# Expert feed-forward on sorted blocks instead of on all experts, in a one-core decoder layer

## The reference

```python
scores = (einsum('btd,ed->bte', x, router_w) + router_b) / max(temperature, 0.1)
gates  = sinkhorn(scores)      # 3 times: subtract logsumexp over experts (-1), then over tokens (-2);
                               # then exp, and divide by the row sum
topk_vals, topk_idx = top_k(gates, 2)
topk_gates = topk_vals / (sum(topk_vals) + 1e-8)
g = relu(einsum('btd,edf->btef', x, wg));  p = einsum('btd,edf->btef', x, wp)
all_out = einsum('btef,efd->bted', g * p, wo)
expert_out = sum(take(all_out, topk_idx) * topk_gates)
x = layernorm(x + (x + expert_out))
```

## Time and profile before

| | |
|---|---|
| median of the runs | 1088.37 us |
| span of the profiled execution | 1083.9 us |
| PE busy | 1014.5 us (94%), 7692 matmuls |
| DVE busy | 775.1 us (72%) |
| ACT busy | 701.3 us (65%) |
| POOL busy | 514.4 us (47%) |
| DMA moved | 14.46 MB, mean 13 GB/s |

### The profile page before, as it was taken

The page is one execution under the profiler, slowest core; times in us unless marked ns, Lnnn a source line. Parts: engine busy times, 40 slices in busy tenths (PEclk is TensorE's granted clock), DMA queues, the critical chain, the costliest instruction groups (busy, mean ns, idle before and its releaser), DMA issues. The chain is left out here.

```text
span 1083.9 us, 24953 instructions
## 1 busy us (share of the span) xinstructions
PE 1014.5 (94%) x7692; PEld 821.1 (76%) x7692; DVE 775.1 (72%) x2061; ACT 701.3 (65%) x2313; POOL 514.4 (47%) x777
## 2 busy tenths in 40 slices
PE   5999999999999999999999999995399999999996
PEld 3677777777778777777777777773288888888886
DVE  3688888888888888888888888885386445544554
ACT  4787888878888788888888888872832222222221
POOL 4744565455654556545665456630323233323333
PEclk9999999999999999999999999996599999999999
DMA  4000000000000000000000000000300000000000
GB/s 116 9 8 11 8 12 7 7 10 7 12 7 7 10 10 10 7 7 10 11 9 7 7 10 10 5 2 0 117 1 10 1 10 10 10 0 10 10 10 10
DMA packets 22520, 14.46 MB, mean 13 GB/s; under 512 B 3296, under 2 KB 21472, under 8 KB 22240
## 3 DMA queue, kind: packets, MB, share of 16 engines
q1 hardware_dynamic: 22496, 14.15, 4.4%
HBM read 12.05 MB, written 2.10 MB: 13 GB/s over the span
## 5 line engine op out<-in xcount | busy, mean ns | idle before, releaser
L1063 ACT ACTIVATE gs<-ps 128x512 f32<-128x512 f32 x128 | 76.4, 599 | 208.7 <-PE ps L1259 208.7
L409 ACT ACTIVATE prob<-ps,negmax 128x128 f32<-128x128 f32 x512 | 182.1, 420 | 1.2 <-DVE negmax L515 1.2
L417 ACT ACTIVATE xprob<-ps,xmax 128x128 f32<-128x128 f32 x512 | 145.5, 428 | 18.5 <-DVE xmax L515 18.5
L336 POOL TENSOR_TENSOR prob<-prob,recip 128x512 f32<-128x512 f32 x128 | 137.2, 1081 | 35.7 <-DVE recip L520 35.7
L1029 POOL TENSOR_TENSOR acc<-acc,part 128x512 f32<-128x512 f32 x64 | 82.6, 1290 | 143.0 <-DVE part L1192 141.2
L345 POOL TENSOR_TENSOR qk_sin<-qk,sin_sb 128x128 f32<-128x128 f32 x256 | 114.3, 466 | 70.9 <-ACT qk L397 70.5
L409 ACT ACTIVATION_READ_ACCUMULATOR prob<-ps,negmax 128x1 f32 x512 | 133.3, 260 | 0.0
L1267 PEld LDWEIGHTS ps<-fwo_sb,h 128*128 128x128 f32 x1024 | 124.0, 192 | 5.6
L1146 DVE TENSOR_TENSOR h<-ps,gs 128x512 f32<-128x512 f32 x128 | 87.6, 689 | 54.9 <-PE ps L1259 53.8
L1267 PE MATMUL ps<-fwo_sb,h 128*128 128x128 f32 x1024 | 124.4, 275 | 0.0
L360 POOL TENSOR_TENSOR ve<-mv,eps 128x1 f32<-128x1 f32 x64 | 12.1, 189 | 208.3 <-DVE mv L538 208.3
(11 more groups left out here) (163 smaller groups left out, 2396.1 us busy)
## 6 DMA issues: line engine op xcount, KB each, us to landing
xf<-in_x SPq DMA_DIRECT2D x32, 64.0 KB, 1.8
xres<-in_x SPq DMA_DIRECT2D x32, 64.0 KB, 1.7
cx<-in_ctx SPq DMA_DIRECT2D x32, 64.0 KB, 1.8
out_y<-yo SPq DMA_DIRECT2D x8, 256.0 KB, 2.3
fstage<-in_fwg SPq DMA_DIRECT2D x1, 1024.0 KB, 5.2
fstage<-in_fwp SPq DMA_DIRECT2D x1, 1024.0 KB, 7.4
qk<-in_wqkv SPq DMA_DIRECT2D x1, 768.0 KB, 4.6
prob<-in_wqkv SPq DMA_DIRECT2D x1, 768.0 KB, 5.8
```

The costliest lines, as they stand in the source:

```text
L336: nc.gpsimd.tensor_tensor(prob[:, n], prob[:, n], recip[:, n, :, None].broadcast_to([128, 4, S]), ALU.mult).then_inc(normed, 1)
L409: last = nc.scalar.activation(prob[:, n, j, :], bank(name)[:, j * S:(j + 1) * S], ACT.Exp, bias=negmax[:, n, j:j + 1], accum_out=sums[:, n ...
L417: last = nc.scalar.activation(xprob[:, n, g, :], bank(name)[:, g * S:(g + 1) * S], ACT.Exp, bias=xmax[:, n, g:g + 1])
```

## The change

The feed-forward is computed only for the two experts of each token. The 32 batches form three groups of 8, 12 and 12. For each group the router runs by itself (64 or 96 columns, one transpose each way). From the chosen experts it counts: a product with a triangular matrix gives each token's rank within its batch for its expert, one with ones the counts, scans give where each expert's rows begin, rounded up to 128. Each token's row of x2 is scattered twice into a DRAM buffer `placed`, to the rows of its two experts, by an indirect transfer of POOL for each batch and choice. A group of n batches has 2n + 7 blocks of 128 rows, whatever the counts: 23 + 31 + 31 = 85. A block is loaded by SP, transposed by PE, split into high and low parts (ACT, DVE), multiplied with both up weights of its expert (512 columns at once, addressed by a register that PE loads from the table `owner`), relu, product, transposed back, multiplied with wo, and stored to DRAM `answered`. POOL gathers the two answers of each token by indirect transfers; DVE multiplies and adds them, and normalises as before. All of it is written out as straight code, no loop. The routing of groups 1 and 2 is dealt out two stages at a time between the blocks (`ROUTED`), the joining of four batches at fixed blocks (`JOINED`, `FINISHED`).

In the attention phase the split of x2 goes, the weight loads and the clearing of `placed` stand in SP's turn 3, and ACT loads one table set that holds exp and ln before all else. The diff, cut to its core:

```diff
+        plan = Sparse([8, 12, 12])
@@ attention_phase, SP, turn 3
+                if isinstance(s, int) and s == 3:
+                    pair = fw_lo[:].bitcast(F32).rearrange("p (e a f) -> p e a f", e=E, a=2)
+                    for a_, src in enumerate((fwg, fwp)):
+                        sp.dma_start(pair[:, :, a_, :], src.rearrange("p (e f) -> p e f", e=E)).then_inc(f_loaded, 16)
+                    sp.dma_start(fwo_sb[:].rearrange("p (n d) -> p n d", d=D), fwo.rearrange("(n p) d -> p n d", p=128))\
+                        .then_inc(fo_loaded, 16)
+                    sp.wait_ge(const_ready, 5)
+                    for rows in placed:
+                        n = rows.shape[0] // 128
+                        sp.dma_start(rows.rearrange("(n p) d -> p n d", p=128), zeros[:, None, :].broadcast_to([128, n, D]))\
+                            .then_inc(cleared, 16)
@@ ACT
+            nc.scalar.preload_act_table_set("natural_log_exp_and_others")
@@ DVE
-                    split_x2(s, c)
                     add_bias(s, c)
@@ ffn_phase
+        ROUTED = {}
+        for k in range(20, STAGES):
+            ROUTED.setdefault((k - 20) // 2, []).append((1, k))
+        for k in range(STAGES):
+            ROUTED.setdefault(11 + k // 2, []).append((2, k))
+        JOINED = {0: 33, 1: 40, 2: 64, 3: 71, 4: 78}
+        FINISHED = {0: 37, 1: 44, 2: 68, 3: 75, 4: 82}
@@ SP
+            def load(i):
+                g, p = plan.group_of[i], i % NX
+                if i == plan.block0[g]:
+                    sp.wait_ge(scattered[g], 16 * 2 * plan.size[g])
+                wait(sp, xt_filled, i - NX + 1)
+                sp.dma_start(xg[p][:], placed[g][at_row:at_row + 128, :]).then_inc(xg_loaded[p], 16)
+            def store(i):
+                sp.wait_ge(y_done, i + 1)
+                sp.dma_start(answered[g][at_row:at_row + 128, :], ysb[i % NY][:]).then_inc(y_stored[i % NY], 16)
+            for i in range(3):
+                load(i)
+            for i in range(NB):
+                if i >= 2:
+                    store(i - 2)
+                if i + 3 < NB:
+                    load(i + 3)
+                ...
@@ POOL
+            def dispatch(g):
+                pool.wait_ge(cleared, 16 * G)
+                pool.wait_ge(rt_dve, dve_after(g, SLOT))
+                for b in range(plan.size[g]):
+                    for k in range(2):
+                        nc.gpsimd.indirect_dma_start(
+                            placed[g], bass.IndirectOffsetOnAxis(place[g][:, k, b:b + 1], 0), x2_all[:, plan.first[g] + b, :], None,
+                            bounds_check=plan.blocks[g] * 128 - 1, oob_is_err=False).then_inc(scattered[g], 16)
+            def gather(q):
+                g, b = plan.quads[q]
+                if b == plan.first[g]:
+                    for p in range(NY):
+                        pool.wait_ge(y_stored[p], 16 * stores_before(p, plan.block0[g] + plan.blocks[g]))
+                wait(pool, acc_step, 3 * (q - 1))
+                for j in range(FB):
+                    for k in range(2):
+                        nc.gpsimd.indirect_dma_start(yg[q % 2][:, k, j, :], None, answered[g], ...)
+            dispatch(0)
+            dispatch(1)
+            gather(0)
+            gather(1)
+            rstd(0)
+            rstd(1)
+            dispatch(2)
+            for q in range(2, len(plan.quads)):
+                ...
@@ ACT
+            split_x(0)
+            for i in range(NB + 1):
+                if i + 1 < NB:
+                    split_x(i + 1)
+                if i < NB:
+                    relu(i)
+                if i >= 1:
+                    hidden_back(i - 1)
+                for g, k in ROUTED.get(i, ()):
+                    route(g, k)
@@ DVE
+            for k in range(STAGES):
+                route(0, k)
+            for k in range(20):
+                route(1, k)
+            split_x(0)
+            for i in range(NB + 2):
+                if i + 1 < NB:
+                    split_x(i + 1)
+                if i < NB:
+                    hidden(i)
+                if i >= 2:
+                    answer(i - 2)
+                for g, k in ROUTED.get(i, ()):
+                    route(g, k)
+                ...
+            for q in range(len(JOINED), len(plan.quads)):
+                join(q)
+                if q > len(JOINED):
+                    normalise(q - 1)
+            normalise(len(plan.quads) - 1)
@@ PE
+            def x_transpose(i):
+                p = i % NX
+                pe.wait_ge(xg_loaded[p], 16 * (i // NX + 1))
+                wait(pe, lo_done, i)
+                nc.tensor.transpose(ps[:, XT, 0:128], xg[p][:], ident[:]).then_inc(xt_filled, 1)
+            def expert_up(i, at_col):
+                pe.wait_ge(lo_done, i + 1)
+                wait(pe, h_done, i - 1)
+                dst, p = ps[:, UP[i % 2], :], i % 2
+                hi, lo = fw_hi[:, bass.ds(at_col * 2, 2 * FF)], fw_lo[:, bass.ds(at_col * 2, 2 * FF)]
+                nc.tensor.matmul(dst, x_lo[p][:], hi, start=True, stop=False)
+                nc.tensor.matmul(dst, x_hi[p][:], hi, start=False, stop=False)
+                nc.tensor.matmul(dst, x_hi[p][:], lo, start=False, stop=True).then_inc(up_filled, 1)
+            x_transpose(0)
+            for i in range(NB + 2):
+                if i < NB:
+                    ...
+                    owners[i] = pe.value_load(owner[g][0:1, j:j + 1], min_val=0, max_val=(E - 1) * FF)
+                    if i + 1 < NB:
+                        x_transpose(i + 1)
+                    expert_up(i, owners[i])
+                if 1 <= i <= NB:
+                    hidden_back(i - 1)
+                if i >= 2:
+                    expert_down(i - 2, owners.pop(i - 2))
+                for g, k in ROUTED.get(i, ()):
+                    route(g, k)
```

699 lines of the change are left out of this document (407 added, 292 removed).

## The result

The changed kernel takes 1186.55 us (median of 4 runs, 1182.43 to 1191.15) against 1088.86 for the kernel before: a ratio of 1.091, 95% interval [1.088, 1.094]. The profiled execution has a span of 1180.6 us. One later run of the kernel before took 1441.17 us at a mean granted clock of 0.65; it is left out of every ratio here. The forecast was 1079, range 1030 to 1160: it named the wrong side, and the time lies outside the range.

What follows compares the result with a forecast made beforehand. PE was taken to bound attention and dense feed-forward. After the logits, 44.2 + 232.5 + 41.1 = 317.8 us against 325.5 before, less 2 of attention: span 1074.2, plus 4.5 outside it, forecast 1079 us, range 1030 to 1160.

Steps and rivals of the forecast that it cites:

- Attention: Attention stretch: DVE loses the copy and subtraction splitting x2 per batch, 2 us less; queued loads and clears cost 0.
- Head: From last logits to first block: routing chain 22.8 us, 16 scatters 17.6, landing 2.0, first load 1.8; 44.2 us.
- Splitting the weights: Head: splitting on ACT, four times about 1 us, with POOL subtractions of 2.3 us each, fits into the chain's waits.
- A block: One block of 128 rows: a chain over five queues, 2.3 us taken, against 1.48 us of PE array time.
- second path: Block, through PE's queue: issuing about 1.2 us, then the expert's register load at 1.1; 2.3 us.
- Loop: All 85 blocks: 195.5 us, drain turns 3, joins 15, routing 12, late scatters 7; 232.5 us.
- Tail: After the blocks: store landing, 24 gathers at 26.4 us, a wait of 1.2, landing, join, normalising, store; 41.1 us.
- POOL rival: Head, tail and blocks: indirect transfer costs above 1.1 us, 88 us for each us; at 1.7, 1132 us; chance 0.25.
- clock rival: Blocks: PE's clock stays at the low level after the head, 1149 us; chance 0.21.
- fast rival: Blocks and transfers: register load and transfers answer sooner, 1.95 us a block, transfers at 1.0; 1048 us; chance 0.09.
- memory path: Block: from x's arrival through answer store to the load queued behind it, 4.4 us shared by two blocks; 2.2 us.

Runs made afterwards that it cites:

- e_lead: Changed kernel with loads up to six blocks ahead instead of three and seven row buffers instead of four, transfers unpaced: 1091.73 us (one run).
- plain-transfer kernel: Changed kernel with every indirect transfer replaced by a plain GpSimd one of 64 KB, fixed rows, so no placing by expert: 1076.97 us (one run).
- b_table: Kernel before with only the combined exp and ln activation table, loaded once at the start: 1082.4 us, ratio 0.996.
- m3: Test kernel without the layer: m1's buffers kept in place, stages varying source, target, operands, semaphores and spacing of transfers: 457.4 us.
- m3b: m3 unchanged, a second time, on m1's first chip: 567.1 us against 457.4.
- e_warm: e_paced with two extra matmuls of 512 columns per block into an unread bank: 1128.66 us against 1130.62 (one run).
- m1: Test kernel without the layer: ten stages of 44 matmul products, each beside one other activity such as scatters, gathers or plain transfers: span 470.1 us.
- m1c: m1 unchanged, a third time, on m1's first chip: 473.9 us.
- m1b: m1 unchanged, once more, on a fourth chip: span 472.0 us against 470.1.
- a3: Changed kernel unchanged, a third time, on a fifth chip: 1183.74 us.
- m2: Test kernel without the layer: ten stages as in m1 but longer, on another chip: no stage held up, no total time given.
- e_paced: Changed kernel with indirect transfers of groups 1 and 2 and first five gathers let go in pairs by finished blocks: 1130.62 us, ratio 1.040.
- e_final: e_lead with indirect transfers beside blocks four at a time, group 2's scatters before second gathers, group 1's routing three stages a block: 1100.53 us, ratio 1.012.
- e_lead2: e_lead unchanged, a second time, on m1's first chip: 1155.97 us against 1091.73.

## Why the prediction was wrong, step by step

Forecast span 1074.2, measured 1180.6: the forecast was 106.4 us too low. The step that failed is the loop: it gave the indirect transfers beside blocks no price on TensorE, and they cost about 77 to 79 us there.

**Attention** (-2): the last logits are done at 759.7 instead of 756.4 (758.4 before); +3.3 us.

**Head** (44.2): 48.7. The chain to the first scatter took 25.3 instead of 22.8; the 16 scatters 20.6 instead of 17.6 (1.29 us each); landing and load 2.8 instead of 3.8. Splitting the weights did hide. +4.5.

**A block** (2.3): right, 2.35, and for the reason given first, the load queued behind the store on SyncE. The second path was mis-sized. With loads earlier, PE's next transposes in e_lead are

```profile
971.60 0.29 PE L1481 MATMUL ps<-ident,xg 128*128 128x128 f32 x1
...
973.32 0.30 PE L1481 MATMUL ps<-ident,xg 128*128 128x128 f32 x1
...
975.01 0.29 PE L1481 MATMUL ps<-ident,xg 128*128 128x128 f32 x1
```

1.70 us apart, PE busy 16.99 of 17 us: array time 1.48 as reckoned, and 0.2 for all that the register load adds, where the prediction had put 1.1 behind 1.2 us of issuing. So 2.3 was right for one path and by luck for the other. That the two paths came out alike hid that one of them could be moved by an edit in SyncE's order, worth 21 us.

**Loop** (232.5): 320.1 from the first transpose to the last answer's store. The plain-transfer kernel has 243.6 by the same count, so blocks, joins and routing were 11 us low together. Within that, errors cancel: its 84 turns at 2.35 us are 197; the five turns with joins (4.1 to 5.0 us) add 11 where 15 were forecast; no scatter is late where 7 us were forecast (its transfers are shorter); and the 29 us that remain go mostly with the routing, which was sized 12. (In e_lead a turn with a join takes 5.1 us against 1.7.) The other 77 us (320.1 less 243.6; 79 by the gaps) are the step that isn't there: for the transfers beside blocks the sum priced only whether they come in time. That the reasoning asked of them when they end and never what they do to TensorE is the failure.

**Tail** (41.1): 52.1. The 24 gathers take 33.1 instead of 27.6 (1.30 each, the wait of 1.2 as reckoned, some of them slowed to 1.06 to 1.41 us). The rest is the last 6 us, in which the program waits for GpSimd's drain. The plain-transfer kernel and e_lead show the same drain of 10.3 us and the same 6 us after their last stores; b_table, without transfers from GpSimd, has 1.1 us and 0.4. So the drain is a price of GpSimd's transfers, plain ones too; but that it shows after the last store depends on when GpSimd finishes. In m3 and m3b, where the drain (8.2 us) has ended before the last store lands, the span ends 0.4 us after that store. In all +11.0.

Sum: 3.3 + 4.5 + 87.6 + 11.0 = 106.4.

**The rivals.** The POOL rival's size was far too large (1.28, not 1.7); by its own formula 1.28 gives 1079 + 16 = 1095, and it did say that from 1.21 on the kernel is slower than before. It is right in sign, and its cause is real but worth 16 us of the 108; the clock rival's 1149 lies nearest by number, and that is luck. Where TensorE isn't held up, 79 us less than 1186.55 would be 1108: inside the range, slower than before; that is an estimate from the gaps, as no run of the changed kernel fell on such a chip. The clock rival falls, though the levels of the earlier trace rows came again: granted 1.00 in undisturbed stretches (1015 to 1031 us), and e_warm raises it without effect. Low clocks (0.53 from 847 to 874 us) come with the gaps and don't make them: in m1 the clock was still 1.00 when TensorE was first held up. The fast rival fell with the pitch of 1.28.

The Trainium skill (DMA: Bandwidth & Descriptors, Anatomy of one DMA) has about 2.0 us and the bytes for a transfer from GpSimd; the page of m1's profile shows 2.2 us to landing for the scatters and 1.8 for plain ones, so it agrees. The time for which GpSimd itself is held, 0.97 and 0.54 us, is what the sum needed.

**Settled and open.** Shown: trains of indirect transfers at a pitch of 1.28 us delay TensorE's instructions, from 7 to 19 us after they start, on three chips (m1 and m1c's, m1b's, a3's) in every program with such trains and in each of its runs; on two others (m2's, m3 and e_lead's) they don't. m3 and e_lead, each run on a chip of either kind, show that it is not the program. What kept TensorE free on held-up chips is a wider spacing: pairs let go by finished blocks (e_paced), four and a break (1.71 us a transfer on average, m3b and e_final), or each waiting for the one two before (1.67, m1). Whether the length of a train or its mean rate decides was not separated. "Chip" stands for all that went with it, the core and the hour too: only the first chip was used twice (held up both times), that m2's does nothing rests on m2 alone, and the chip of the changed kernel's first runs isn't on record. Not shown: why. All runs here, the timed ones too, come with the profiler's records, so that its recording takes part can't be excluded. The Trainium skill (NOTIFIC — the notification-queue block, 7.1 Overflow) says that inside the block which writes these records the pipeline always pushes back rather than lose one (what a full ring in memory does is another setting). A queue that fills for some microseconds and then paces each instruction would look like the hold-up, but this is a guess: no run here turned the records off, and why it would be TensorE's alone is unexplained.

## What to carry to other kernels

Before rows are moved by indirect transfers beside a dense engine, look at how densely they come: at most four back to back, then a wait until they have landed, kept TensorE free here and, with earlier loads and a better order, took 83 us off this kernel. Where a store and the load of a later block share a queue, the load's lead is a free knob: price the block as if the load were early before accepting the memory path as its bound. A gain of 167 us of array time was given back by 40 serial transfers at 1.3 us, by block chains, by 21 padded blocks and, on some chips, by the hold-up; and one part of the change alone, the single table, is faster than both kernels, by 0.4% and 9%. Where GpSimd starts transfers, let it finish its work early enough: the drain lasts 9.2 us beyond its last operation here, and hides only behind other work.

## What the runs showed of the hardware

- An indirect transfer of 128 rows of 512 bytes holds GpSimd 0.97 us (scatter) or 1.00 (gather), with 0.30 until the next; a plain one 0.54. Rows of 128 bytes cost the same (pitch 1.28 in m2), 32 rows instead of 128 hardly less (1.17).
- The same program differs by 64 us (e_lead 1091.73, e_lead2 1155.97) and m3 by 110 us between chips, while the kernel before stays between 1083.9 and 1089.9 on all of them, but for its one run of 1441.17. One kernel measured on one chip wasn't enough here.
- A train of indirect transfers at a pitch of 1.28 to 1.30 us holds TensorE up on some chips from 7 to 19 us after its start; at 1.67 to 1.71 us on average it did not. Under the hold-up TensorE's instructions come at multiples of about 0.7 us, while DVE, ScalarE and the transfers themselves keep their pace.
- In programs in which GpSimd starts transfers, its drain at the end takes 10.3 us (8.2 in m1 and m3) instead of 1.1; in the changed kernel the program ends 6 us after its last store for that.
